# Weight conversion of a transformer layer: its loads and casts put on GpSimd instead of ScalarE and VectorE

## The reference

```python
x = layernorm(x + attn(x, Wq, Wk, Wv, Wo, mask))   # 16 heads, log-sigmoid mask of 2048 x 2048 per head
x = layernorm(x + ffn(x))                          # attention with q_w, k_w, v_w, gate_w, out_w, then 8 experts

logits = xr @ moe_gate_w + moe_gate_b
chosen = jnp.max(jax.lax.top_k(logits, 2)[1], axis=-1)
hh = gelu(_ln(xr @ W1 + B1, G, Bt))                # for every expert: W1 1024 x 2048, W2 2048 x 1024
outs = (hh @ W2 + B2) * rsc + xr                   # of which each token takes that of its chosen expert
```

## Time and profile before

| | us |
|---|---|
| median of 3 runs | 26514.12 |
| lowest and highest of them | 26426.17, 27034.49 |
| the profiled execution, its own time | 26451.57 |
| its span, slowest core (0) | 26450.0 |
| spans of the eight cores | 26370.4 to 26450.0 |

### The profile page before, as it was taken

The page is one execution under the profiler, slowest core; times in us unless marked ns, Lnnn a source line. Parts: engine busy times, 40 slices in busy tenths (PEclk is TensorE's granted clock), DMA queues, the critical chain, the costliest instruction groups (busy, mean ns, idle before and its releaser), DMA issues.

```text
span 26450.0 us, 127157 instructions; the slowest of 8 cores (26370.4 to 26450.0 us)
## 1 busy us (share of the span) xinstructions
PE 12357.2 (47%) x39075; PEld 3524.3 (13%) x39664; DVE 4858.3 (18%) x8163; ACT 5621.4 (21%) x6163; POOL 472.6 (2%) x885
## 2 busy tenths in 40 slices
PE   0003333343335555556566545656545554656653
PEld 0000000000001111112222211111111111222221
DVE  1110000000001111232222231111122123222223
ACT  0002222222222222212222221222222221222222
POOL 0110000000000000000000000000000000000000
PEclk9997555555555555578888865555555557888886
DMA  4442222222221000000101101111100000111010
GB/s 130 153 144 81 92 90 78 79 75 92 91 83 47 3 3 3 2 25 28 34 29 30 34 18 55 46 47 48 34 4 3 4 1 23 31 34 29 27 36 19
DMA packets 625875, 1244.29 MB, mean 47 GB/s; under 512 B 57142, under 2 KB 262080, under 8 KB 625218
## 3 DMA queue, kind: packets, MB, share of 16 engines
q1 hardware_dynamic: 272546, 692.86, 8.7%
q0 software_dynamic: 104608, 371.25, 3.5%
q10 hardware_dynamic: 248064, 172.01, 2.2%
HBM read 864.71 MB, written 371.20 MB: 47 GB/s over the span
## 4 chain that ended last, share of the span: by engine, by line
PE 40%; ACT 19%; DMA 18%; DVE 14%; issue 8%; DVEq 1%; ACTq 0%; SPq 0%; POOLq 0%; another core or an unknown queue 0%; POOL 0%; PEldq 0%
ACT pb L589 7%; PE psA L830 7%; PE psC L592 7%; PE psC L890 6%; DMA mln<-mz 4%; PE psB L582 4%; DMA wbf_w<-hhB 4%; DVE psA L605 3%; DMA mz<-mln 3%; PE psA L582 3%; DMA sig<-mz 3%; PE psA L586 2%; PE psB L586 2%; ACT mz L478 2%; DVE sh L848 2%
## 5 line engine op out<-in xcount | busy, mean ns | idle before, releaser
L592 PE MATMUL psC<-pb,vab 128*65 128x512 bf16 x4096 | 2116.8, 620 | 2693.4 <-ACT pb L589 2693.4
L830 PE MATMUL psA<-xA,wk 128*128 128x512 bf16 x7986 | 2132.6, 414 | 501.8 <-DMA wk<-wbf_w 469.4
L601 DVE CAST ao<-psC 64x2048 bf16<-64x2048 f32 x64 | 146.1, 2283 | 7890.6 <-PE psC L592 7890.6
L582 PE MATMUL psA<-qk 64*128 64x512 bf16 x2048 | 1054.1, 617 | 686.4 <-DVE rowb L606 596.2
L455 PE MATMUL psA<-mz,E 128*8 128x512 bf16 x32 | 16.2, 608 | 2768.8 <-ACT xB L454 2768.8
L589 ACT ACTIVATE pb<-psA,cc 128x1024 bf16<-128x1024 f32 x512 | 569.9, 1113 | 2472.7 <-PE psA L586 2472.7
L582 PE MATMUL psB<-qk 64*128 64x512 bf16 x2048 | 1056.1, 618 | 0.0
L890 PE MATMUL psC<-ao,hhB 128*128 128x512 bf16 x4012 | 943.6, 391 | 112.1 <-ACT hhB L875 106.5
L830 PEld LDWEIGHTS psA<-xA,wk 128*128 128x128 bf16 x8192 | 765.3, 104 | 1644.2 <-issue 1040.6
L592 PEld LDWEIGHTS psC<-pb,vab 128*65 128x65 bf16 x4096 | 384.7, 143 | 4488.3 <-issue 4488.3
L589 ACT ACTIVATE pb<-psB,cc 128x1024 bf16<-128x1024 f32 x512 | 569.9, 1113 | 1646.3 <-PE psB L586 1646.3
(11 more groups left out here) (295 smaller groups left out, 13500.3 us busy)
## 6 DMA issues: line engine op xcount, KB each, us to landing
mz<-mln SPq DMA_DIRECT2D x512, 512.0 KB, 3.2
wk<-wbf_w SPq DMA_DIRECT2D x640, 256.0 KB, 2.6
wst<-w ACTq DMA_DIRECT2D x512, 256.0 KB, 3.2
sig<-mz POOLq DMA_DIRECT2D x256, 512.0 KB, 2.9
mz<-sig SPq DMA_DIRECT2D x256, 512.0 KB, 3.9
mln<-mz POOLq DMA_DIRECT2D x256, 512.0 KB, 4.7
wbf_w<-hhB POOLq DMA_DIRECT2D x256, 256.0 KB, 3.7
ao<-wbf_w SPq DMA_DIRECT2D x256, 256.0 KB, 2.7
```

What stands on the lines that cost most here:

```text
L582: smm = [p.on("tensor", lambda e, kc=kc, half=half, j=j, ps=ps, rb=rb: e.matmul(ps[:, 512 * j:512 * (j + 1)], qk[rb:rb + 64, 2048 + 128 * ...
L592: vmm = [p.on("tensor", lambda e, kc=kc, half=half, j=j, vo=vo: e.matmul(psC[0:65, 1024 * half + 512 * j:1024 * half + 512 * (j + 1)], vab ...
L830: mm = [p.on("tensor", lambda e, a=a, base=base, tc5=tc5, psl=psl: e.matmul(psl, wk[:, base + 128 * a:base + 128 * (a + 1)], xA[:, 2048 * ...
```

## The change

The loads of the conversion are issued by POOL, and the casts run on POOL. Everything else, the waits asked for, the buffers and the semaphores of the transfers among it, stays as it was.

```diff
             for hf in (0, 1):
                 par = wpp["n"] % 2
                 wpp["n"] += 1
-                tl = p.on("scalar", lambda e, ...: e.dma_start(out=wst[...], in_=src_fn(hf)),
+                tl = p.on("gpsimd", lambda e, ...: e.dma_start(out=wst[...], in_=src_fn(hf)),
                           wait=[wpp[par]], inc=16, sem="cv0" if par == 0 else "cv1", tag="cvd")
                 if scl is None:
-                    ct = p.on("vector", lambda e, ...: e.tensor_copy(hhB[...], wst[...]),
+                    ct = p.on("gpsimd", lambda e, ...: e.tensor_copy(hhB[...], wst[...]),
                               wait=[tl, cvst[par2]], inc=1, tag="cvc")
                 else:
-                    ct = p.on("vector", lambda e, ..., scl=scl: e.tensor_scalar_mul(hhB[...], wst[...], scl),
+                    ct = p.on("gpsimd", lambda e, ..., scl=scl: e.tensor_scalar_mul(hhB[...], wst[...], scl),
                               wait=[tl, cvst[par2]], inc=1, tag="cvc")
```

More of the change, by code:

```diff
@@ L353, in emit_convert @@
                 wpp["n"] += 1
-                tl = p.on("scalar", lambda e, hf=hf, par=par: e.dma_start(out=wst[:, 512 * par:512 * (par + 1)], in_=src_fn(hf)),
+                tl = p.on("gpsimd", lambda e, hf=hf, par=par: e.dma_start(out=wst[:, 512 * par:512 * (par + 1)], in_=src_fn(hf)),
                           wait=[wpp[par]], inc=16, sem="cv0" if par == 0 else "cv1", tag="cvd")
                 if scl is None:
-                    ct = p.on("vector", lambda e, hf=hf, par=par, par2=par2: e.tensor_copy(hhB[:, 1024 * par2 + 512 * hf:1024 * par2 + 512 * (hf + 1)], wst[:, 512 * par:512 * (par + 1)]),
+                    ct = p.on("gpsimd", lambda e, hf=hf, par=par, par2=par2: e.tensor_copy(hhB[:, 1024 * par2 + 512 * hf:1024 * par2 + 512 * (hf + 1)], wst[:, 512 * par:512 * (par + 1)]),
                               wait=[tl, cvst[par2]], inc=1, tag="cvc")
                 else:
-                    ct = p.on("vector", lambda e, hf=hf, par=par, par2=par2, scl=scl: e.tensor_scalar_mul(hhB[:, 1024 * par2 + 512 * hf:1024 * par2 + 512 * (hf + 1)], wst[:, 512 * par:512 * (par + 1)], scl),
+                    ct = p.on("gpsimd", lambda e, hf=hf, par=par, par2=par2, scl=scl: e.tensor_scalar_mul(hhB[:, 1024 * par2 + 512 * hf:1024 * par2 + 512 * (hf + 1)], wst[:, 512 * par:512 * (par + 1)], scl),
                               wait=[tl, cvst[par2]], inc=1, tag="cvc")
```

## The result

| | us |
|---|---|
| before, median of 10 runs | 26497.04 (26421.14 to 27034.49) |
| after, median of 10 runs | 27829.74 (27782.96 to 28066.45) |
| ratio after to before | 1.0516, 95% interval 1.0489 to 1.0543 |
| profiled execution after, spans of the cores | 27746.7 to 27923.4 |

The changed kernel is 5.2% slower, 1333 us by the medians; 27800 was forecast. Where the cores of one die ran longer than those of the other in part of the executions (two of four for the serial order on the old engines, three of four for the first run of the fastest version), the times of the remaining executions stand beside the median.

A forecast was written before the change was run, and what follows sets the result against it. The exposed conversion, paced by a ring of store and cast, was taken as the bound; a call would go from 5.17 to 9.14 us, 328 x 3.97 = 1302 us, less 6, giving 27800 us, range 27120 to 28590.

The forecast's parts named there:

- 1, the store's row: Start of a conversion call on POOL: the row of the previous call's store takes 0.54 us.
- 2, gap before the first load's row: POOL's delay in starting the next issue after the store's row: 0.45 us, between 0 and 0.60.
- 3, first load, beside a store: First load of a call, landing while the old store runs: 3.2 us, bounds 2.3 and 3.7.
- 4, cast: First cast of 512 numbers on POOL: 0.60 us, bounds 0.43 and 1.03.
- 5, gap and second load: After the first cast: the gap again, 0.45 us, then the second load, now alone, 2.7 us.
- 6, cast and 0.60 to the store's row: End of a call: second cast, 0.60 us, then 0.60 us from cast to the store's row.
- the prediction's own signs: Steps fail if POOL's cast isn't 0.6 us, loads miss 2.7 to 3.2, or 512-piece rows exceed 128-piece ones.
- The gain of 6 us at the handing over: First mask store follows the conversion's last store after some 1 us, not 6.97, as ACT is ready beforehand: 6 us.
- Rival A: Conversion calls serial, but with fewer transfers in flight landings are quick; within 2%, below 6.79 us a call; chance 4%.
- Rival B: POOL's load issue grows with 512 pieces, up to 2.16 us, 648 us more; with other costs over 10.3 us, 18%.
- the sum made with that rule (8.44 us a call): Prediction's call sum with 2.6 us for both loads, from the skill's transfer rule; kernel 230 us below the main sum.

The follow-up runs named there:

- the serial order on the old engines: Kernel before, loads on ACT and casts on DVE, with waits forcing the changed kernel's load, cast, load, cast order: 27450.81 us.
- the fastest version: Changed kernel with W1 and W2 behind the masks, attention matrices on ACT and DVE, a store semaphore per place of hhB: 25311.01 us, again 25138.92 us.
- own store semaphores: Kernel before with a separate semaphore for the stores from each of the two places of hhB: 26187.64 us, ratio 0.9872.

## Why the prediction was right, step by step

The mechanism held: the conversion is exposed, POOL runs load and cast in turn, the store is no longer waited for, what lies behind keeps its length. The sum, 9.14 us a call, met 9.42. Its terms did less well than the sum (the last column is the mean over the calls of W1 and W2):

| step of the prediction | predicted | measured (call at 880.34) | mean |
|---|---|---|---|
| 1, the store's row | 0.54 | 0.54 to the next row | 0.59 |
| 2, gap before the first load's row | 0.45 | 0 | in the 0.59 |
| 3, first load, beside a store | 3.2 | 3.83 | 3.71 |
| 4, cast | 0.60 | 0.61 | 0.61 |
| 5, gap and second load | 0.45 + 2.7 | -0.06 + 3.27 | 3.20 in all |
| 6, cast and 0.60 to the store's row | 1.20 | 1.18 | 1.18 |
| sum | 9.14 | 9.37 | 9.29 |

Steps 2, 3 and 5 were wrong, each time a gap and a load in opposite directions. The gap I had put before the load's row, as POOL's own way to start a transfer, appears only when POOL must wait for a semaphore (0.57 us between cast and store); with nothing to wait for, the row nearly always follows at once, and it can even begin 0.06 us before the cast has ended. In exchange both loads land later than I had taken from ACT and SP: 3.83 us from the row to the cast instead of 3.2, and 3.27 instead of 2.7. The errors cancel to 0.2 us in the first load and to 0.1 in the second. That is luck: by the prediction's own signs, a load outside 2.7 to 3.2 us and a longer row with 512 pieces, these steps failed while the sum held. What made the total larger still is the cast with a factor: 32 x 0.87 us = 28 us. The gain of 6 us at the handing over came as predicted.

Rival A, quick landings, was half true and worthless: the store did fall to 2.4 us, but it is not waited for, and the loads did not. Rival B, the pieces of a load, exists in small: the load's row is 0.75 us with 512 pieces and 0.54 with 128 (the next fence, a W2 call), not 2.16. This W2 call took 8.53 us from store to store, the W1 call above 9.37; in the mean over 128 calls of each they take 9.05 and 9.53.

```profile
1043.52 0.55 POOL L364 DMA_DIRECT2D wbf_w<-hhB  x1 [0.56 <-POOL hhB L357]
1044.05 0.54 POOL L354 DMA_DIRECT2D wst<-w  x1
1047.42 0.61 POOL L357 CAST hhB<-wst 128x512 bf16<-128x512 f32 x1 [2.83 <-DMA wst<-w]
1047.98 0.54 POOL L354 DMA_DIRECT2D wst<-w  x1
1050.88 0.61 POOL L357 CAST hhB<-wst 128x512 bf16<-128x512 f32 x1 [2.37 <-DMA wst<-w]
1052.05 0.55 POOL L364 DMA_DIRECT2D wbf_w<-hhB  x1 [0.56 <-POOL hhB L357]
```

Of the two rules of the Trainium skill, the one on POOL's arithmetic ("GPSIMD Engine Reference", section "Elementwise — side-by-side cycle accounting") fits in its easy case for the plain cast: 613 ns for 512 numbers stay below its 769 ns, and from the 195 ns of 128x16 the slope is 0.84 ns a number. The operation with a factor, 1480 ns, lies far above both of its cases. With 2.0 us plus bytes over 436 GB/s ("DMA: Bandwidth & Descriptors", section "Anatomy of one DMA — SWDGE (gpsimd) path") a 256 KB transfer takes 2.6 us, as an estimate; the store has 2.4, but the lone loads 2.9 (W2, 1050.88 - 1047.98) and 3.3 us (W1) in these calls, 3.1 and 3.4 in the mean. So for loads the measurement decides, and the sum made with that rule (8.44 us a call) would have been too low.

What stays open: why a lone load issued by POOL is there later than one issued by ACT in the serial order, by 0.18 us for W2 and 0.38 for W1 in the means over all calls. The difference between the two, 0.2 us, is about that between POOL's rows for 512 and for 128 pieces (0.75 and 0.54). A run with nothing but lone loads from each engine was not made. Of the 1.10 us between the store's row and the first cast, the run with the load ahead of the store gave back only a part, since another wait took its place, so what that place in the order costs by itself was not measured either.

## What to carry to other kernels

Where an engine issues each load just ahead of the operation that consumes it, it can't load ahead: in an in-order list the next issue stands behind the wait. Look at the order first, the engine's speed second: moving two loads ahead of two casts gave back 3.0 of 4.25 us, with every instruction still on the slow engine. And ask of an exposed stage whether it has to stand there: the same slow work on the idle engine, put beside a stage that doesn't need that engine, cost the path next to nothing and made the kernel 3.8% faster than before, and 5.3% together with the attention matrices back on ACT and DVE and a store semaphore for each place of `hhB`.

## What the runs showed of the hardware

- POOL casts 128x512 from float32 to bf16 in 0.613 us, but the same size with a factor takes 1.48 us; DVE takes 0.43 for either.
- An issue on POOL begins 0.57 us after the end of the operation whose semaphore it waits for, and nearly always at once (0.54 after the start of the row before) when it waits for nothing.
- When a store lands goes with its place among the loads. Issued ahead of the loads in flight with it, it lands in 2.4 us in the median, with one load behind it (the changed kernel) and with two (only the loads on POOL; both loads ahead). Issued behind a load, it takes 3.1 us (serial order on the old engines), 3.3 (load ahead of the store) and 3.5 to 3.7 (the kernel before, only the casts on POOL, own store semaphores). Why is not shown.
- POOL's loads went through its queue as far fewer packets than ACT's: the queues' lines over the conversion, after (first), against the earlier trace rows:

```profile
q0 software_dynamic: 77600, 254.34, 25.7%
```

  77,600 packets for loads and stores together, against 248,064 for ACT's loads and 26,240 for the stores, and 25.7% of the engines' time over 3050 us against 46.9% over 1700, which is 784 against 797 us. Fewer packets saved the transfer engines next to no time and brought no earlier landing.
